# Column norms of the masked scores taken for two sets per stationary operand, in a graph-attention plus gated-recurrence kernel

## The reference

```
h = relu(layernorm(x))
q, k, v = h Wq^T, h Wk^T, h Wv^T
rel = adj^T * (q k^T)                      # 64 x 64 per graph
rel = rel / norm(rel, over its last axis)
x = x + rel v
h = relu(layernorm(x))
3 times: a = adj h ; z, r = sigmoid(...) ; hv = tanh(a W5 + (r*h) U5) ; h = (1-z) h + z hv
out = x + h
```

## Time and profile before

| | |
|---|---|
| median of 3 executions | 982.24 us (981.36 to 982.58) |
| the profiled execution | 981.1 us, of which the span is 978.8 us |
| PE, matmuls | 960.0 us busy, 98% of the span |
| PE, loads of stationary operands | 829.2 us, 85% |
| DVE | 678.8 us, 69% |
| ACT | 501.1 us, 51% |
| POOL | 119.8 us, 12% |
| granted clock of PE, mean | 0.992 of full speed |

### The profile page before, as it was taken

The page is one execution under the profiler, slowest core; times in us unless marked ns, Lnnn a source line. Parts: engine busy times, 40 slices in busy tenths (PEclk is TensorE's granted clock), DMA queues, the critical chain, the costliest instruction groups (busy, mean ns, idle before and its releaser), DMA issues.

```text
span 978.8 us, 15089 instructions
## 1 busy us (share of the span) xinstructions
PE 960.0 (98%) x5256; PEld 829.2 (85%) x5256; DVE 678.8 (69%) x1338; ACT 501.1 (51%) x877; POOL 119.8 (12%) x161
## 2 busy tenths in 40 slices
PE   7799999999999999999999999999999999999996
PEld 7788888888888888888888888888888888888885
DVE  4866768776677776877767767776768766676644
ACT  4455554645446463554725645356544555445542
POOL 1210112102030010200102001110111101020000
PEclk9899999999999999999999999999999999999998
DMA  5011111211022020310203102031010311010001
GB/s 168 1 44 44 39 48 41 90 43 64 21 71 87 13 86 0 128 43 0 86 17 111 43 0 86 21 107 43 25 60 21 107 43 57 28 58 28 1 2 43
DMA packets 41537, 49.43 MB, mean 51 GB/s; under 512 B 4400, under 2 KB 37936, under 8 KB 41520
## 3 DMA queue, kind: packets, MB, share of 16 engines
q1 hardware_dynamic: 41520, 49.20, 15.3%
HBM read 26.12 MB, written 23.07 MB: 50 GB/s over the span
## 4 chain that ended last, share of the span: by engine, by line
PE 96%; DVE 1%; ACT 1%; issue 0%; POOL 0%; DVEq 0%; POOLq 0%
PE gate L357 14%; PE gate L359 13%; PE gate L358 13%; PE cand L357 9%; PE cand L359 9%; PE cand L358 9%; PE fea L460 9%; PE tok L453 4%; PE fea L420 3%; PE tok L357 2%; PE tok L358 2%; PE tok L359 2%; PE fea L357 1%; PE fea L358 1%; PE fea L359 1%; PE fea L429 1%
## 5 line engine op out<-in xcount | busy, mean ns | idle before, releaser
L643 ACT ACTIVATE h_hi<-h 128x512 fp32r<-128x512 f32 x92 | 56.6, 633 | 120.3 <-DVE h L1002 92.4
L866 DVE TENSOR_TENSOR d_s<-c_s,h 128x512 f32<-128x512 f32 x96 | 66.4, 705 | 67.3 <-ACT c_s L738 66.9
L719 ACT ACTIVATE r_s<-gate,b_r 128x512 f32<-128x512 f32 x96 | 64.9, 684 | 89.8 <-PE gate L359 89.8
L738 ACT ACTIVATE c_s<-cand,b_c 128x512 f32<-128x512 f32 x96 | 64.8, 684 | 52.9 <-PE cand L359 52.9
L866 DVE TENSOR_TENSOR rh_lo<-rh,rh_hi 128x512 fp32r<-128x512 f32 x96 | 72.3, 792 | 26.4 <-ACT rh_hi L643 25.1
L305 POOL TENSOR_TENSOR rstd<-vare,minus_half 128x4 f32<-128x4 f32 x32 | 33.0, 1032 | 449.7 <-DVE vare L894 449.7
L866 DVE TENSOR_TENSOR a_lo<-fea,a_hi 128x512 fp32r<-128x512 f32 x96 | 64.3, 687 | 34.4 <-ACT a_hi L643 34.4
L357 PE MATMUL gate<-a_hi,W_hi_wz 128*128 128x512 f32 x192 | 79.4, 413 | 0.0
L357 PE MATMUL cand<-rh_hi,W_hi_u 128*128 128x512 f32 x192 | 78.2, 407 | 0.0
L357 PE MATMUL cand<-a_hi,W_hi_w 128*128 128x512 f32 x192 | 78.1, 407 | 0.0
L1008 DVE TENSOR_TENSOR rh<-r_s,h 128x512 f32<-128x512 f32 x96 | 63.6, 681 | 17.6 <-ACT r_s L719 17.6
(11 more groups left out here) (122 smaller groups left out, 2286.6 us busy)
## 6 DMA issues: line engine op xcount, KB each, us to landing
x_s<-x SPq DMA_DIRECT2D x16, 512.0 KB, 5.2
out<-o_s SPq DMA_DIRECT2D x16, 512.0 KB, 3.0
hx_trip<-hx SPq DMA_DIRECT2D x14, 512.0 KB, 2.6
hx_back<-hx_trip SPq DMA_DIRECT2D x56, 128.0 KB, 2.8
h_trip<-h_blk SPq DMA_DIRECT2D x14, 512.0 KB, 2.6
h_back<-h_trip SPq DMA_DIRECT2D x56, 128.0 KB, 2.8
z_s<-w_t SPq DMA_DIRECT2D x1, 512.0 KB, 4.1
r_s<-w_t SPq DMA_DIRECT2D x1, 512.0 KB, 5.0
```

The lines of the kernel that those rows point to most:

```text
L643: return nc.scalar.activation(dst, src, ACT.Copy)
L719: nc.scalar.activation(r_s[:, c, :], gate[:, c, :], ACT.Sigmoid, bias=b_r[:, c:c + 1]).then_inc(r_ready, 1)
L738: nc.scalar.activation(c_s[:, c, :], cand[:, c, :], ACT.Tanh, bias=b_c[:, c:c + 1]).then_inc(c_ready, 1)
L866: return nc.vector.tensor_tensor(dst, a, b, ALU.subtract)
```

## The change

`sq` keeps only the diagonal quarters: for each set 64 columns in place of 128, where partitions 0 to 63 hold the first graph's squares and partitions 64 to 127 the second graph's. Two sets then fill one stationary operand of 128 columns. What moves is a new constant `of_half`, 128 partitions by two columns, whose first column is one on the lower 64 partitions and zero on the upper ones, and whose second column is the reverse. A matmul gives 128x2: row `a * 64 + n` is node n of set `2b + a`, column e is graph e of the set. The squares are two ACT instructions of 64 partitions by 256 elements. The copy to `norm2` has to undo the layout, and is four DVE copies of 64 partitions by two elements, two of which go from one half of the partitions to the other. DVE sets `of_half` with four memsets at the program's start. `of_half` is declared last of the tensors in SBUF; `sq` is 1 KB per partition smaller, so the small tensors declared behind it lie 1 KB lower. Nothing else is moved or changed.

```
-        sq = sb("sq", [P, Q, P])
+        sq = sb("sq", [P, Q, N])
...
         rnorm = sb("rnorm", [P, Q])
+        of_half = sb("of_half", [P, 2])
...
+        def half(e):
+            return slice(e * N, (e + 1) * N)
...
                 pe.wait_ge(sq_ready, g + 1)
                 fea_wait(n_fea, 1)
-                for q in range(Q):
-                    last = nc.tensor.matmul(fea[:, 1, q:q + 1], sq[:, q, :], ones[:], start=True, stop=True)
+                for b in range(HQ):
+                    two = sq[:, 2 * b:2 * b + 2, :].rearrange("p q n -> p (q n)")
+                    last = nc.tensor.matmul(fea[:, 1, 2 * b:2 * b + 2], two, of_half[:], start=True, stop=True)
                 last.then_inc(fea_full, 2)
...
                 copy(S_hi[:], S[:]).then_inc(S_hi_ready, 1)
-                nc.scalar.activation(sq[:], S[:], ACT.Square).then_inc(sq_ready, 1)
+                for e in range(2):
+                    last = nc.scalar.activation(sq[half(e), :, :], S[half(e), :, half(e)], ACT.Square)
+                last.then_inc(sq_ready, 1)
...
                 fea_wait(n, 1)
-                nc.vector.tensor_copy(norm2[:], fea[:, 1, 0:Q]).then_inc(fea_taken, 2)
+                for e in range(2):
+                    for a in range(2):
+                        last = nc.vector.tensor_copy(norm2[half(e), :].rearrange("p (b a) -> p b a", a=2)[:, :, a],
+                                                     fea[half(a), 1, 0:Q].rearrange("p (b e) -> p b e", e=2)[:, :, e])
+                last.then_inc(fea_taken, 2)
...
             dve.sem_inc(h_lo_new, 4)
+            for e in range(2):
+                for a in range(2):
+                    nc.vector.memset(of_half[half(a), e:e + 1], 1.0 if a == e else 0.0)
```

## The result

The changed kernel takes **973.41 us** (median of 4 executions, 972.4 to 973.88), the kernel before, run beside it, 982.41 (981.36 to 982.75). The ratio is 0.9909, with a 95% interval of 0.9892 to 0.9926. The profiled execution took 973.88 us, its span is 971.6, and the mean granted clock 0.994. The ratios are the recorded ones; they are not the quotients of the medians and can differ from them by some 0.001.

A forecast was written before the change was run, and what follows sets the result against it. PE, busy without a wait at full clock in the seven rounds, was taken as the bound. The loop's -6.2 us and the start's +0.1 sum to -6.1, so 982.24 becomes 976.1 us, with a range of 974.5 to 979.5.

The forecast's parts named there:

- The loop: PE's norms in the rounds: four of eight loads go, saving 0.45 us a group, 6.2 us in 14 groups.
- The squares: On ACT, one square becomes two: the pair takes 0.62 us in place of 0.52, +0.10 us.
- the slack: Ahead of PE's norms in the rounds: the squares have 0.34 us to spare, so ACT's added 0.10 fits.
- The copies: On DVE, one copy becomes four: the three added cost between 0.21 and 0.48 us, and 0.48 was taken.
- DVE's cover: Windows 5 of group Y and 3 of group X: DVE's added 0.48 us costs PE nothing in the rounds.
- the tightest place: Window 5 of group Y: the second `rh` still moves with PE, with 0.21 us left over.
- The start: Before the rounds: the second group's norms start 0.10 + 0.48 us later and take 0.45 less, +0.1 us.
- 1: Squares come late at PE's norms: ACT's pair takes the upper bound, +0.46 us; time 978.2, chance 0.07.
- 2: Window 5 of Y: copies and power delay `x_s` by over 0.69 us, PE's gain there is lost; 979.2, chance 0.07.
- 3: PE's norms: time from first load to next work stays at 1.01 us, no change; 982.2, chance 0.04.
- 4: Norms' wait for squares: PE idles some 0.83 us, the granted clock falls, 35 us added; 1011, chance 0.04.

The follow-up runs named there:

- PE's part alone: Kernel before with only two two-column matmuls for four one-column ones, squares and copy unchanged: 988.83 us with `ones2` ahead of the large tensors, 975.07 with it last.
- the filled pair: Kernel before and changed kernel, each with products nobody reads put into PE's idle stretches of the start: 978.64 and 972.4 us.
- DVE's part alone: Kernel before with only the copy to `norm2` made four copies between the halves, matmuls and squares as before: 982.45 us, ratio 0.9998.
- both costs: Kernel before with two squares and four copies, matmuls as before: 983.97 us, ratio 1.0003.
- `fp32r`: Changed kernel with the squares and the two columns of `of_half` as fp32r, one load and matmul per product in place of two: 973.52 us, ratio 0.9906.
- ACT's part: Kernel before with only the square made two instructions of 64 partitions by 256 elements, matmuls and copy as before: 982.84 us, ratio 1.0013.

## Why the prediction came out as it did

**The loop, right.** 14 x 0.45 = 6.2 us was forecast. 6.5 was measured between the two profiles, 6.3 (0.90 x 7) from PE's part alone and from the filled pair. The remaining 0.03 a round I can't place; rounds of kernels that should agree with the one before differ by as much (117.67 to 117.71). The 0.111 us a load is right to 0.006. Moving two columns in place of one changed nothing: four loads in 0.52 us in the start, less one duration of 0.19, over three steps, is 0.11 us again.

**The squares, mis-sized.** "The pair takes 0.62 in place of 0.52, +0.10 us" is the first term that failed: it measured +0.34. The duration, 0.41, was right. The step "or 0.31 from start to start" assumed that two half-wide squares overlap by the 0.10 that the full-width one overlaps with its neighbour, and they don't. The number of elements is not the reason: the Relu of 256 elements on all 128 partitions does overlap, with 0.49 from start to start at a duration of 0.60. Left are the 64 partitions and the step from one half to the other, and which of them it is was not tried. It cost the rounds nothing, because the slack held with 0.13 us left, and the start 0.24 us more than forecast.

**The copies, right, and DVE's cover too.** +0.48 was forecast and +0.50 measured. For the operation right behind them it is 0.59 (0.70 in place of the 0.11 of the earlier trace rows): with DVE's part alone it starts 0.03 us after the end of the fourth copy, where it started 0.05 ahead of the end of the one; that cost nothing either. The second `rh`, named as the tightest place, moved with PE, with 0.18 us left where 0.21 had been expected.

**The start, wrong twice.** "They start 0.10 + 0.48 later and take 0.45 less: **+0.1 us**". The chain is 1.00 us longer, of which the squares explain 0.34, the copies 0.50 and POOL's power 0.13, for which the prediction had no term. Less the 0.47 of the shorter norms this term should be +0.53. It alone would have moved the forecast away from the result, to 976.6. The step of the prediction that failed, and took the measured time out of the range, is a term that the sum put at nothing: the granted clock in the start. The prediction computed 1.7 us for one fall and used it for a rival only, which asked whether a fall would be added and never whether one would go missing. The spread of executions in its range came from three of them, which lay within 1.2 us. The kernel before has three such stretches in its profile. In the profiles of this record the one from 45 us on comes in single length, in double length or not at all, worth up to 2.9 us of time. A range of 974.5 to 979.5 around 976.1 left no room for it going missing: seven of the 16 executions of the changed kernel lie in the range, the nine with a clock of 0.994 or more all below it, and the first four were all of the nine. With the measured 6.5 and 0.53, 982.24 becomes 976.3, which is next to the mean of the upper seven, 976.35. Over all 70 and 16 executions the means are 982.0 and 974.5, a difference of 7.5 us.

At equal clock, the change is worth 5.7 to 6.3 us, where 6.1 was forecast. That this fits so well is in part luck: the loop gained 0.3 more than forecast, and the start cost 0.4 more.

**The rivals.** 1: ACT's pair came to three quarters of its bound (0.34 of 0.46 on ACT, 0.21 in when the squares are ready), and `fea<-sq` is no wait in the loop. 2: refuted, see `rh`. 3: refuted, 0.56 in place of 1.01. 4: refuted, the clock is 1.00 from 60 to 960 us; a fall does matter, but in the start, and by being absent.

**What stays open.** The changed kernel has the high clock more often than the kernel before (9 of 16 executions against 5 of 66), and that is where the means differ by 7.5 us and not by 6. The kernel with DVE's part alone has it in 6 of 12. How the delays of the copies bring that about is open: the profiled executions of the kernels with DVE's part, with both costs and with `fp32r` show the fall at double length, so the change doesn't exclude it.

## What to carry to other kernels

Where PE is busy without a wait at full clock, count its loads: each one taken off was worth its distance to the next here, 0.11 us, and the work moved to other engines was free (rounds of 117.67 us with ACT's part and 117.69 with DVE's, 117.71 before), with 0.13 us of slack left ahead of the norms; measure such slack against the upper price. Read the clock of every idle stretch before forecasting to a few microseconds, and the mean clock of every execution when comparing two kernels: a start whose clock falls by chance, here to 0.57 over 4 us or not at all, is a term of the sum with a spread of its own. Dummy products in the idle took away most of the spread here and brought 3.0 us. And a new small tensor is declared behind the large ones, or padded to 64 bytes (1.5 us here, against 14.0 with 8), since its place alone cost more here than the change brings.

## What was not expected of the hardware

Where a small tensor is declared changes PE's pace. With one of 8 bytes a partition ahead of the large activation tensors, a product of 512 columns takes 0.233 us from load to load in place of 0.227, and the whole kernel 996.21 us in place of 982.22, with no wait of PE in the rounds. It shows in three kernels (the pad, PE's part alone with 988.83 us, and the changed kernel with `of_half` ahead with 990.0), and goes away when the tensor is moved behind the others (975.07 for PE's part alone), or all but 1.5 us of it when the pad has 64 bytes. In the products of weights the moving operand alone is declared behind it; no kernel moved one tensor by itself, and why it matters is open.

Two ACT instructions, on one half of the partitions each, don't overlap as full-width neighbours do: 0.41 and 0.44 us from start to start at a duration of 0.41, where the full-width Square of 0.617 has 0.52.

Whether PE's clock falls in the start differs between executions of one kernel, and the odds differ between kernels: with the four small copies of DVE 20 of 48 executions had a mean clock of 0.993 or more, and without them 7 of 102.
